# One PSUM region and three copies for a pair's queries, keys and values in the tail pipeline

## What is computed

```python
Q = linear(layernorm(x), Wq, bq); K = linear(ctx, Wk, bk); V = linear(ctx, Wv, bv)   # 16 heads of 8
corr = irfft(rfft(Q) * conj(rfft(K)))            # along the sequence
corr_mean = corr.mean(axis=-1)                   # over the 8 of a head
top_w, top_idx = top_k(corr_mean, 4)             # int(log(65)) = 4 delays
out = sum_i softmax(top_w)[i] * roll(V, top_idx[i])
x = x + linear(out, Wo, bo)
x = x + ternary_ffn(layernorm(x))                # needs max |xn| over everything
```

## Time and profile before

| | |
|---|---|
| time, median of 3 | 1307.05 us (1306.04 to 1310.28) |
| profiled execution | 1308.58 us, of which the span of the trace is 1306.8 us |
| busy over the span | PE 95%, PEld 77%, DVE 82%, ACT 70%, POOL 58% |
| `tail` in the trace | from 1105 to 1278.7 us, some 173 us |
| `ternary` in the trace | from 1278.7 us to the end |

### The profile page before, as it was taken

One profiled execution on the slowest core, in us unless ns is written; L12 is line 12 of the kernel. 1 busy time (PEld: TensorE's weight loads), 2 busy tenths in 40 slices (PEclk: granted clock), 3 DMA queues, 4 the chain that ended last, 5 costly groups with the idle time before them and its releaser, 6 DMA issues. The chain is left out here.

```text
span 1306.8 us, 29951 instructions
## 1 busy us (share of the span) xinstructions
PE 1245.4 (95%) x9114; PEld 999.9 (77%) x9114; DVE 1070.6 (82%) x2050; ACT 918.6 (70%) x1555; POOL 761.2 (58%) x817
## 2 busy tenths in 40 slices
PE   6999999996999999999999999999999999898986
PEld 4777777774788887787878878787888887787865
DVE  5878888885988988979977988879988976688887
ACT  4778888884777776777677677777677776876740
POOL 3766666562665665665656666656665623576670
PEclk9999999997999999999999999999999999999998
DMA  5411010101977776776777777767777784100004
GB/s 125 110 29 30 28 32 28 32 16 28 219 181 174 179 177 161 187 171 162 179 175 171 177 177 162 184 168 166 189 174 176 183 186 107 39 28 25 18 1 129
DMA packets 126150, 159.57 MB, mean 122 GB/s; under 512 B 20840, under 2 KB 59504, under 8 KB 126064
## 3 DMA queue, kind: packets, MB, share of 16 engines
q1 hardware_dynamic: 124974, 158.16, 50.1%
q10 hardware_dynamic: 1090, 0.43, 0.1%
HBM read 152.25 MB, written 6.29 MB: 121 GB/s over the span
## 5 line engine op out<-in xcount | busy, mean ns | idle before, releaser
L1036 DVE TENSOR_TENSOR e_m<-e_pu,raw 128x1024 f32<-128x1024 f32 x256 | 309.9, 1211 | 95.5 <-ACT e_pu L1099 67.8
L1099 ACT ACTIVATE e_pu<-e_pu 128x1024 f32<-128x1024 f32 x256 | 258.6, 1010 | 161.1 <-PE e_pu L1135 158.9
L1109 ACT CAST e_mh<-e_m 128x1024 fp32r<-128x1024 f32 x256 | 268.1, 1047 | 47.5 <-DVE e_m L1036 46.0
L955 POOL TENSOR_TENSOR e_ml<-e_m,e_mh 128x1024 fp32r<-128x1024 f32 x80 | 193.0, 2415 | 125.3 <-ACT e_mh L1109 125.1
L1041 DVE TENSOR_TENSOR e_ml<-e_m,e_mh 128x1024 fp32r<-128x1024 f32 x176 | 238.7, 1356 | 21.6 <-ACT e_mh L1109 20.9
L1133 PE MATMUL e_pu<-r_xh,wuh 128*128 128x512 f32 x528 | 215.2, 408 | 2.8 <-PEq L208 1.9
L1144 PE MATMUL e_py<-e_mh,wdh 128*128 128x512 f32 x528 | 208.4, 395 | 3.0 <-ACT held L1086 3.0
L1134 PE MATMUL e_pu<-r_xh,wul 128*128 128x512 f32 x528 | 209.3, 396 | 0.0
L1135 PE MATMUL e_pu<-r_xl,wuh 128*128 128x512 f32 x528 | 209.3, 396 | 0.0
L1145 PE MATMUL e_py<-e_mh,wdl 128*128 128x512 f32 x528 | 209.2, 396 | 0.0
L1148 PE MATMUL e_py<-e_ml,wdh 128*128 128x512 f32 x528 | 168.2, 397 | 1.0 <-DVE e_ml L1041 0.4
(11 more groups left out here) (228 smaller groups left out, 2356.8 us busy)
## 6 DMA issues: line engine op xcount, KB each, us to landing
raw<-gates_scratch SPq DMA_DIRECT2D x512, 256.0 KB, 4.3
x_res<-in_x_dram SPq DMA_DIRECT2D x64, 64.0 KB, 1.8
xcT<-in_ctxT_dram SPq DMA_DIRECT2D x64, 64.0 KB, 2.0
held<-in_ctx_dram SPq DMA_DIRECT2D x32, 128.0 KB, 2.1
out_dram<-t_res SPq DMA_DIRECT2D x16, 256.0 KB, 2.3
raw<-in_L_ffn_W_up_dram SPq DMA_DIRECT2D x4, 512.0 KB, 4.3
raw<-in_L_ffn_W_down_dram SPq DMA_DIRECT2D x4, 512.0 KB, 5.9
gates_scratch<-raw SPq DMA_DIRECT2D x16, 128.0 KB, 2.3
```

What stands on the lines that cost most here:

```text
L955: nc.gpsimd.tensor_tensor(flat(ml[k][:]), flat(m[k][:]), flat(mh[k][:]).bitcast(F32), ALU.subtract).then_inc(m_low[1], 1)
L1036: nc.vector.tensor_tensor(flat(m[r % 3][:]), flat(pu[r % 3][:]), flat(gt[i % SPREAD]), ALU.mult).then_inc(gated, 1)
L1099: nc.scalar.activation(flat(pu[k][:]), flat(pu[k][:]), ACT.Silu).then_inc(silued, 1)
L1109: nc.scalar.copy(flat(mh[k][:]), flat(m[k][:])).then_inc(m_high, 1)
```

## The change

The two PSUM tensors of `pq` become one that covers both tiles, each tile in a bank of its own. ACT copies both tiles together: one copy of 128 x 2 x 384 and two of 64 x 2 x 128, in place of six. `projected` and `q_out` are raised once a pair. PE waits for `q_out` ahead of the first tile for the whole pair before, and ACT for `projected` until both tiles are there. On ACT the `cf` copy, which stood between the two tiles, now stands ahead of them.

```diff
-        pq = [psum(f"l_pq{i}", [P, 3, D]) for i in range(2)]
+        pq = psum("l_pq", [P, 2, 512])[:, :, 0:3 * D].rearrange("p j (c d) -> p j c d", d=D)
...
-                        pool.wait_ge(q_out, 2 * n + 2)
+                        pool.wait_ge(q_out, n + 1)
...
-                        at_least(act, projected, 2 * (n - 1))
+                        at_least(act, projected, n - 1)
...
-                    for j in range(2):
-                        if on(s, 2):
-                            n = s - 2
-                            at_least(act, mixed, n - SLOTS + 1)
-                            at_least(act, products, n - SLOTS + 1)
-                            act.wait_ge(projected, 2 * n + j + 1)
-                            nc.scalar.copy(qkv[:, n % SLOTS, j, 1:4, :], pq[j][:])
-                            nc.scalar.copy(qkv[S:, n % SLOTS, j, 0, :], pq[j][0:S, 1, :])
-                            nc.scalar.copy(qkv[0:S, n % SLOTS, j, 0, :], pq[j][S:, 1, :]).then_inc(q_out, 1)
-                        if g is not None and j == 0:
-                            act.wait_ge(c_transformed, g + 1)
-                            at_least(act, mixed, 4 * (g - 1))
-                            nc.scalar.copy(cf[:, g % 2].rearrange("p i t h -> p i (t h)"), pab).then_inc(c_out, 1)
+                    if g is not None:
+                        act.wait_ge(c_transformed, g + 1)
+                        at_least(act, mixed, 4 * (g - 1))
+                        nc.scalar.copy(cf[:, g % 2].rearrange("p i t h -> p i (t h)"), pab).then_inc(c_out, 1)
+                    if on(s, 2):
+                        n = s - 2
+                        at_least(act, mixed, n - SLOTS + 1)
+                        at_least(act, products, n - SLOTS + 1)
+                        act.wait_ge(projected, n + 1)
+                        nc.scalar.copy(qkv[:, n % SLOTS, :, 1:4, :], pq)
+                        nc.scalar.copy(qkv[S:, n % SLOTS, :, 0, :], pq[0:S, :, 1, :])
+                        nc.scalar.copy(qkv[0:S, n % SLOTS, :, 0, :], pq[S:, :, 1, :]).then_inc(q_out, 1)
...
-                    for j in range(2):
-                        if on(s, 2):
-                            n = s - 2
-                            pe.wait_ge(f_out, n + 1)
-                            at_least(pe, q_out, 2 * n + j - 1)
-                            nc.tensor.matmul(pq[j][:, 0, :], xf[:, n % 2, j, 0, :], cst["w1T"][:, 0, :], start=True, stop=False)
...
+                    if on(s, 2):
+                        n = s - 2
+                        pe.wait_ge(f_out, n + 1)
+                        at_least(pe, q_out, n)
+                        for j in range(2):
...
+                            nc.tensor.matmul(pq[:, j, 0, :], xf[:, n % 2, j, 0, :], cst["w1T"][:, 0, :], start=True, stop=False)
...
+                        ins.then_inc(projected, 1)
```

More of the change, by code:

```diff
@@ new lines, in _ @@
+                    if on(s, 2):
[3 more added lines that the diff above has]
+                        for j in range(2):
+                            if g is not None and j == 1:
+                                pe.wait_ge(w_out, g + 1)
+                                at_least(pe, c_out, g)
+                                for i in range(2):
+                                    ins = nc.tensor.matmul(pab[:, i, :], cst["dft"][:, i * P:i * P + P], cT[:], start=True, stop=True)
+                                ins.then_inc(c_transformed, 1)
+                            nc.tensor.matmul(pq[:, j, 0, :], xf[:, n % 2, j, 0, :], cst["w1T"][:, 0, :], start=True, stop=False)
+                            nc.tensor.matmul(pq[:, j, 1:3, :], xf[:, n % 2, j, 1, :], cst["w1T"][:, 1:3, :], start=False, stop=False)
+                            ins = nc.tensor.matmul(pq[:, j, 0:2, :], cst["first_rows"][:], cst["bias3"][:, 0:2, :], start=False, stop=True)
+                        ins.then_inc(projected, 1)
+                    elif g is not None:
+                        pe.wait_ge(w_out, g + 1)
+                        at_least(pe, c_out, g)
+                        for i in range(2):
+                            ins = nc.tensor.matmul(pab[:, i, :], cst["dft"][:, i * P:i * P + P], cT[:], start=True, stop=True)
+                        ins.then_inc(c_transformed, 1)
```

## The result

| | before | after |
|---|---|---|
| median of 18 runs each | 1308.32 us | 1312.7 us |
| lowest and highest | 1302.56 to 1310.96 | 1307.94 to 1315.58 |
| profiled execution, span of the trace | 1308.58, 1306.8 | 1311.21, 1309.4 |
| first `pq` to the first product of `ternary` | 170.57 | 176.80 |

The two medians lie 4.4 us apart. The ratio over all runs is 1.0037 [1.0026, 1.0048], which is 4.8 us. Ratios are taken without the one slow run on record, of the kernel before beside `c0` to `e6`: 1716.59 us at a mean granted clock of 0.654. The two spans differ by only 2.6 us, because the untouched part ahead of `tail` was 3.45 us shorter in the trace of after (first `pq` at 1104.91 for 1108.36). So the stages are compared from the first `pq` on: +6.2 us.

A forecast was written before the change was run, and what follows sets the result against it. The period's chain, through PE, ACT's copies, `pp` and DVE's full list, was taken as the bound. Opening 2.3, periods 2.91 and neighbours 0.5 gave +5.7 us, from 1307.05 to 1312.8, range 1308.0 to 1317.5.

The forecast's parts named there:

- The copies: On ACT: wide copy 800 ns, half copies 369 ns each, three in 1.55 us for 2.00, saving 0.45 a pair.
- a page's rule: ACT's copies by the skill's price, 186 ns + 0.833 an element, 93 overlap: 1.44 us, total some 1.5 us less.
- When the copies end: ACT's `qkv` copies start only after tile 1, so they end 0.26 us later, in W 0.43 us later.
- PE's wait for `z_out`: PE's `pt` waits for ACT's scaling into `xnT`: 0.23 us in A and another 0.23 in B.
- The period: From `pw` to `pw`: A's `q_out` and all behind it 0.49 us later; first period 0.26, four at 0.49.
- such neighbours: POOL's work falls later against DVE's list in B and C: 0 to 0.3 us a period, 0.5 in all.
- The 0.69 behind the last pair: After the last pair that passes `pq`, 0.43 + 0.26 = 0.69 us of delay stays.
- The opening: Single `pq` sets the pace before the first `po`: 3.37 us a pair for 2.73; 2.3 us in all.
- rival 2: PE's 0.23 us waits vanish in its wait for `w`; only the opening pays: 1308 to 1310, chance 0.22.
- rival 3: New pauses let the granted clock fall in more periods, 1.77 us each: two more 1316.3, three 1318; chance 0.16.
- rival 4: Two-bank copies are cheap, under 1.29 us for the three, so `q_out` comes earlier: 1306.4 or 1303; chance 0.06.

The follow-up runs named there:

- c0: The kernel before, run once more with no edit; 1305.85 us for 1308.00 beside it, ratio 0.9987.
- e6: The kernel before, with ACT's scaling into `xnT` moved ahead of the cT, `cf` and `qkv` copies; 1307.20 us, ratio 0.9994 to before.
- a1: The changed kernel, run once more with no edit; 1313.9 us for 1307.38 of before, ratio 1.0053.
- e3: The changed kernel, but pairs 0 to 9 with the copies, waits and order of before; 1309.51 us, ratio 1.0019 to before.
- e8: The changed kernel, with POOL's `pp` of a marking step waiting for DVE's norm of the weighing step; 1308.26 us, ratio 1.0006 to before.
- e1: The changed kernel, with ACT's scaling into `xnT` moved ahead of the `cf` and `qkv` copies; 1310.68 us, ratio 1.0030 to before.
- e7: The kernel before, with POOL's `pp` of a marking step waiting for DVE's norm of the weighing step; 1300.48 us, ratio 0.9940 to before.
- e2: The changed kernel, with six copies in place of three but still one buffer and one wait for the pair; 1317.03 us, ratio 1.0079 to before.
- e5: The changed kernel, with pairs 0 to 9 as before, then wide copies per tile, joined half copies, and scaling first; 1301.31 us, ratio 0.9945 to before.
- e4: The changed kernel, with a wide copy for each tile started when that tile is there, half copies joined; 1301.79 us, ratio 0.9957 to before.
- e9: The kernel of `e5`, with POOL's `pp` of a marking step waiting for DVE's norm of the weighing step; 1299.21 us, ratio 0.9937 to before.

## Why the prediction came out

The time, 1312.8 predicted and 1312.7 measured, is closer than its terms were. Point by point:

- **The copies: right.** Wide copy 0.80 us, half copies 0.364 and 0.369, by line and form in the trace of after (minimum, median, maximum in ns):

```profile
L1513 ACT COPY l_qkv<-l_pq x32: 782/799/801, 1106.6 to 1253.6; 128x768 f32<-128x768 f32 x32
L1514 ACT COPY l_qkv<-l_pq x32: 364/364/366, 1107.5 to 1254.4; 64x256 f32<-64x256 f32 x32
L1515 ACT COPY l_qkv<-l_pq x32: 369/369/372, 1107.8 to 1254.8; 64x256 f32<-64x256 f32 x32
```

  Three end 1.56 us after the first starts (1210.00 to 1211.56). Of the two prices weighed under "a page's rule", the one from the rows held: by the page's, the three would have ended after 1.44 us. The overlap that the Trainium skill, "ScalarE: Activation LUTs", section "What ACT_TABLE_LOAD costs", gives for neighbours is not seen between these copies. It is seen behind them: the scaling (1211.59 + 0.56) ends 0.10 us after the next copy has started (1212.05).
- **When the copies end: right in kind.** In W they end 3.99 us after `pw` (1211.56), and I had 3.98 (1208.10 to `pw` at 1204.12).
- **PE's wait for `z_out`: right in A and in B.** A's `pt` is 0.24 us later (predicted 0.23). B's is another 0.35 in the period shown, where the first `pq` products behind the wait took 0.46 us in place of 0.39; but that is the one exception. In the four other periods of this trace, and in those of `a1`, `e3` and `e8`, the products take 0.39 and B's `pt` is another 0.21 to 0.26 later (predicted 0.23). That these waits lengthen the period was argued, and is not shown (`e1`).
- **The period: the chain right, one term mis-sized.** In the usual period, that of `a1`, the top values are 0.52 us later (predicted 0.49). The rest, 0.26, comes behind them, in DVE's full list: the norm in C takes 1.17 us beside `pp`, for 0.92 before. `pp` in C is 0.78 us later and the norm only 0.52, so the norm waits longer for `pp` to end. Together 0.78 in `a1`, 0.76 in `e8` against `e7`. For such neighbours I had taken 0.5 us in all five periods; it is 0.25 in each. Over the five, 0.26 + 4 x 0.49 + 0.5 = 2.7 us were predicted, and 0.5 + 4 x 0.78 = 3.6 measured (the last of the four as `e8` against `e7`, 18.80 for 18.02, since before has 0.91 there). The 0.69 behind the last pair came out: 0.68, in after and in `e8` against `e7` (16.97 for 16.29).
- **The opening: mis-sized.** Predicted 2.3 us, measured 3.6, and `e3` took 3.5 of it back. Two small terms in a loop that runs once a pair: from the copy's end to PE it is 0.14 us (1108.20 to 1108.34), where I had taken POOL's 0.08; and the 0.07 on the first product. The pairs are 3.51 us apart and not 3.37. The first `ext` is 2.42 us late (predicted 2.0), and of this nothing was won back before the first `pw`, where I had taken off 0.4: it is 2.43 late.
- **Hidden (rival 2): wrong.** `e3` has the opening of before, and its full-clock periods are still 0.76 us longer (20.35 for 19.59). PE's wait for `w` has stayed at 1.99 us in after although PE came later: DVE came later by as much.
- **The clock (rival 3): not the cause.** Means of 0.92 stand in two middle periods of after, and 0.90 in the stretch 1246.82 to 1263.78; before has 0.92 in one middle period and 0.91 in two of the later stretches. `e2` is slower than after, and all its middle periods are at 1.00. Over all its runs after has a mean clock of 0.986 (18 runs), before 0.984 (the 23 beside `a1`): the change doesn't lose by the clock, it gets a little back. The Trainium skill, "TensorE: Matmul & The Clock Gate", section "A second HAM failure mode: psum-queue depth-cycling", tells of a kernel that cycles through PSUM banks and whose small idles between groups of products made the clock go up and down. It says nothing of a single buffer. In the traces, the waits of 0.84 us in the opening left the clock at 1.00, and the opening is where this buffer binds.
- **Faster (rival 4): wrong.** The three copies take 1.56 us, more than the 1.29 at which it turns.

So the number was in part luck. Stage by stage, at a clock of 1.00 on both sides, the change costs 3.6 (opening) + 0.5 + 4 x 0.78 + 0.7 = 7.9 us. My terms added to 5.7, with 1.3 us too little in the opening and 0.8 in the neighbours. Two things hid this. The forecast started from 1307.05, the median of three runs, where the 18 runs gave 1308.32, so 1312.7 is only 4.4 us above. And the clock gives back: from the first `pq` on, the two traces lie 6.2 us apart and not 7.9. At equal mean clock, `e8` against `e7`, the medians lie 7.8 us apart. What is left of the gap in the first measurement is not settled: `c0` shows that a tenth of a per cent comes and goes between sets of runs, and the first `pq` comes at 1104.9 to 1109.3 us in the traces, ahead of any line that was changed.

What I had missed altogether is the collision of the norm with `pp`. It is in the trace of before as well, and in a period it is worth more than the change, 1.05 us for 0.78. I had seen it at `zn` (1.24 us for 0.59) and priced it as a slowing of up to 0.3 us, where it is a turn that one of the two loses.

## What to carry to other kernels

Joining two copies saves the fixed cost of each, but the joined one starts when the last producer is done: if its end feeds the chain, compare the ends, not the sums. A buffer that is filled and emptied in turn is a loop; count in it every hand-over, in both directions, because each is paid once a turn. And where an instruction of DVE or POOL on the chain has two durations in the trace, look for the other engine's instruction beside it before anything else: one wait that fixes who goes first gave as much here as the best edit to the copies (`e7` 0.9940, `e5` 0.9945).

## What the runs showed of the hardware

- **Some DVE and POOL instructions take turns.** The same two DVE tensor_scalar take 0.59 to 0.60 us alone, and 1.56 to 1.57 when a 1.27 us POOL tensor_tensor starts 0.2 us behind the first: the second ends when POOL has. No semaphore stands between the two in the kernels before and after, so the engines wait for one another in this way too, and the profile books it as duration. In `e4` neighbouring periods differ by 0.94 us, and POOL starts 0.21 or 0.85 us behind the norm. The scaling of `w` (L1389, both inputs in SBUF) takes 0.69 us beside POOL's `rr` and 0.29 alone. Not every DVE instruction is held: the addition of `py` out of PSUM (L1427) takes 0.41 us with `pp` beside it or without. The Trainium skill, "SBUF — State Buffer", section "Who interferes with whom", says that a DVE instruction in a 2-port mode, which tensor_scalar can enter, contends with GpSimd for a shared port pair, which whoever issues first has for the whole instruction. The trace agrees, 0.60 against 1.57; no row shows the mode itself.
- **A copy out of two banks costs what its length says.** 799 ns for 768 elements lie on the line through 372 for 256 and 479 for 384.
- **The granted clock.** Among the middle periods, a mean of 0.92 or 0.93 stood only in those ahead of which PE had waited 2.0 to 2.3 us for `w`, but not in all of these (`e3` has three at 1.00). In `e7`, `e8` and `e9`, where that wait is at most 0.94 us, none of them fell below 1.00. Near the end of `tail` it is not so: after has 0.90 from 1246.82 on, behind a wait of 0.41 us.
- **A gain of 0.6%.** The fastest, `e9`, is 0.9937 [0.9921, 0.9954] of before; `e7`, before with the one wait, 0.9940 [0.9924, 0.9956]. The two can't be told apart, and `e7` has one edit. A part of both is the clock.
